# Cross-attention and feed-forward kernel on one core: a new order of its on-chip buffers, with the large ones meant to begin at multiples of 2048 bytes

## The reference

```python
x1 = layernorm(layernorm0(x), ln1_g, ln1_b)       # layernorm0: no gain, no bias
x2 = layernorm(ctx_768, ln2_g, ln2_b)
q, k, v = x1 @ Wq + bq, x2 @ Wk + bk, x2 @ Wv + bv
attn = softmax(einsum('bqe,bke->bqk', q, k) * 512 ** -0.5)
x = x + einsum('bqk,bke->bqe', attn, v) @ Wo + bo
# feed-forward; w_fc (2048 x 512), w_proj (512 x 2048), u, v of rank 16
def bitlinear(x, w):                              # ternary weights with one scale per row
    scale = max(mean(abs(w), axis=1), 1e-05)
    return x @ (clip(round(w / scale), -1, 1) * scale).T
n = layernorm0(x)
h = bitlinear(n, w_fc) + gate * (n @ v.T @ fast_b.T @ u.T)
return x + bitlinear(max(h, 0) ** 2, w_proj)
```

## Time and profile before

| | us |
|---|---|
| median of 3 runs | 861.97 |
| the 3 runs | 861.27, 861.97, 862.39 |
| time of the profiled execution | 861.97 |
| its span, from first to last instruction | 860.2 |

### The profile page before, as it was taken

One profiled execution on the slowest core, in us unless ns is written; L12 is line 12 of the kernel. 1 busy time (PEld: TensorE's weight loads), 2 busy tenths in 40 slices (PEclk: granted clock), 3 DMA queues, 4 the chain that ended last, 5 costly groups with the idle time before them and its releaser, 6 DMA issues.

```text
span 860.2 us, 11132 instructions
## 1 busy us (share of the span) xinstructions
PE 837.7 (97%) x4232; PEld 682.2 (79%) x4232; DVE 559.6 (65%) x1143; ACT 328.2 (38%) x639; POOL 137.3 (16%) x124
## 2 busy tenths in 40 slices
PE   5999789999999999999999999999999999999997
PEld 3758678888888888888888888888888888888885
DVE  4898685376836786477836786476836786476434
ACT  2687234332434234332434234333434234323332
POOL 1102140012300150012300150012300150013001
PEclk9999989999999999999999999999999999999999
DMA  9653101010111011010101011010101010000001
GB/s 326 159 151 96 38 1 49 1 37 16 41 44 37 0 50 50 1 37 24 41 35 38 1 50 50 0 37 25 53 23 37 1 49 1 1 1 25 26 0 50
DMA packets 19513, 36.55 MB, mean 42 GB/s; under 512 B 6898, under 2 KB 6898, under 8 KB 19460
## 3 DMA queue, kind: packets, MB, share of 16 engines
q1 hardware_dynamic: 18004, 35.84, 12.5%
q10 hardware_dynamic: 1456, 0.01, 0.1%
HBM read 27.45 MB, written 8.39 MB: 42 GB/s over the span
## 4 chain that ended last, share of the span: by engine, by line
PE 93%; DVE 4%; DMA 1%; issue 1%; ACT 0%; SPq 0%; POOL 0%; DVEq 0%; ACTq 0%
PE H L1114 28%; PE O L1096 27%; PE G L1014 24%; PE G L1040 3%; PE H L1120 3%; PE H L1014 1%; PE H L1040 1%; PE G L1069 1%; DMA Wk_s<-in_L_xattn_Wk_dram 1%; PE H L978 1%; PE H L998 1%; PE H L1003 0%; PE O L1135 0%; PE O L1137 0%; DVE below L913 0%
## 5 line engine op out<-in xcount | busy, mean ns | idle before, releaser
L1114 PE MATMUL H<-xnT,fcT 128*128 128x512 f32 x1024 | 263.2, 399 | 0.0
L1096 PE MATMUL O<-projT,qbuf 128*128 128x512 f32 x1008 | 257.9, 398 | 0.0
L1114 PEld LDWEIGHTS H<-xnT,fcT 128*128 128x128 f32 x1024 | 188.7, 188 | 41.9
L1096 PEld LDWEIGHTS O<-projT,qbuf 128*128 128x128 f32 x1008 | 186.3, 188 | 41.5
L646 ACT ACTIVATE qbuf<-rbuf 128x512 fp32r<-128x512 f32 x128 | 80.8, 631 | 165.5 <-DVE rbuf L887 86.5
L891 DVE TENSOR_TENSOR qbuf<-rbuf,qbuf 128x512 fp32r<-128x512 f32 x128 | 97.1, 758 | 55.6 <-ACT qbuf L646 55.6
L887 DVE TENSOR_TENSOR rbuf<-rbuf 128x512 f32<-128x512 f32 x128 | 105.6, 825 | 42.4 <-ACT rbuf L640 40.7
L640 ACT ACTIVATE rbuf<-H,scf 128x512 f32<-128x512 f32 x128 | 87.2, 681 | 93.0 <-PE H L1120 92.2
L525 POOL TENSOR_TENSOR xrs<-xrs,mhalf 128x4 f32<-128x4 f32 x9 | 9.4, 1040 | 365.1 <-DVE xrs L853 365.1
L1014 PE MATMUL G<-n1T,M 128*128 128x512 f32 x276 | 65.9, 395 | 0.0
L1014 PE MATMUL G<-Wvo,tT 128*128 128x512 f32 x270 | 65.7, 396 | 0.0
(11 more groups left out here) (158 smaller groups left out, 983.3 us busy)
## 6 DMA issues: line engine op xcount, KB each, us to landing
xb<-in_x_dram SPq DMA_DIRECT2D x8, 1024.0 KB
ctxb<-in_ctx_dram SPq DMA_DIRECT2D x8, 768.0 KB
wring<-in_L_ffn_w_fc_dram SPq DMA_DIRECT2D x16, 256.0 KB, 5.8
wring<-in_L_ffn_w_proj_dram SPq DMA_DIRECT2D x16, 256.0 KB, 3.5
out_dram<-x2a SPq DMA_DIRECT2D x8, 512.0 KB, 2.6
out_dram<-x2b SPq DMA_DIRECT2D x6, 512.0 KB, 2.6
Wq_s<-in_L_xattn_Wq_dram SPq DMA_DIRECT2D x4, 256.0 KB, 4.2
Wo_s<-in_L_xattn_Wo_dram SPq DMA_DIRECT2D x1, 1024.0 KB, 15.7
```

Source lines behind the costliest of these rows:

```text
L1096: mm = pe.matmul(banks[f"O{t}"][:, :], qbuf[:, j % 2, h, t * P:(t + 1) * P], projT[:, j, :], start=(j == 0 and h == HI), stop=(j == NFF - ...
L1114: pe.matmul(banks[f"H{j % 2}"][:, :], fcT[:, k, j * P:(j + 1) * P], xnT[:, h, k, :], start=(k == 0 and h == HI), stop=False)
```

## The change

The six large weight buffers, `sprow` and `crow` move from the head of the allocation to behind the small tiles. Between the small tiles and the large ones comes a buffer that nothing uses, `up_to_a_line`, whose length is worked out from where the allocator stands. And `absj`, a buffer of the prologue, is now another view of `sprow` instead of 2048 bytes of its own.

```diff
-        fcT = sb("fcT", [P, KD, HID], F32R)
-        projT = sb("projT", [P, NFF, D], F32R)
-        M = sb("M", [P, 2, KD, DC], F32R)
-        Wvo = sb("Wvo", [P, 2, KC, D], F32R)
-        uT = sb("uT", [P, HID], F32R)
-        FB = sb("FB", [P, KD, P], F32R)
         ident = sb("ident", [P, P])
         identb = sb("identb", [P, P], BF16)
-        sprow = sb("sprow", [P, D])
-        crow = sb("crow", [P, D])
-        bqrow = crow[:, :]
         tbias = sb("tbias", [P, KC])
...
         rinv = sb("rinv", [P, TILES])
+        LINE = 2048
+        sb("up_to_a_line", [P, (-nc.sbuf_base % LINE) // 4])
+        fcT = sb("fcT", [P, KD, HID], F32R)
+        projT = sb("projT", [P, NFF, D], F32R)
+        M = sb("M", [P, 2, KD, DC], F32R)
+        Wvo = sb("Wvo", [P, 2, KC, D], F32R)
+        uT = sb("uT", [P, HID], F32R)
+        FB = sb("FB", [P, KD, P], F32R)
+        sprow = sb("sprow", [P, D])
+        crow = sb("crow", [P, D])
         ctxb = sb("ctxb", [P, TILES, DC])
...
+        bqrow = crow[:, :]
+        absj = sprow[:, :].bitcast(BF16).rearrange("p (a d) -> p a d", a=2)
...
-        absj = sb("absj", [P, 2, D], BF16, setup)
```

## The result

| | before | after |
|---|---|---|
| median of the runs, us | 861.62 (859.85 to 862.39, 4 runs) | 847.55 (845.89 to 848.33, 4 runs) |
| ratio, 95% interval | | 0.984 (0.982 to 0.986) |
| span of the profiled execution, us | 860.2 | 846.1 |

The change made the kernel 1.6% faster.

A forecast was written before the change was run, and what follows sets the result against it. It took TensorE's rate of matmul starts, over 85% of the span, as the bound. The profiled execution's 861.97 us plus 0 for all seven parts gave 862.0 us, range 860.3 to 863.7.

The forecast's parts named there:

- What bounds the kernel: From 118 to 850 us TensorE is always busy, so the rate at which matmuls start sets the time.
- What the change does to addresses: Large buffers land 32 bytes behind multiples of 2048, not on them; three consequences for alignment and relative places follow.
- point (c): Weights and streamed operand of one matmul, 32 bytes apart within 2048 before, now stand equal or whole 512s apart.
- Part 1: Weight group's rest by 64 goes from 0 to 32 in the long matmuls: cost 0, bound 0.8 us each way.
- Part 2: Rows crossing a multiple of 2048: 512 columns still cross, halves of 256 columns swap, so units s swap times; cost 0.
- Part 3: Long matmuls with both operands at the same place: priced from units s and w, of 256 columns, at 0.
- Rival A: Equal operand places slow the long matmuls, by 0.0107 ns a column: 15 us slower, 877 us; chance 0.05.
- Rival B: The long matmuls' 20 ns over their columns are a collision the new places avoid: 56 us faster, 806 us; chance 0.02.
- Parts 4 to 7: VectorE and GpSimd with sprow and crow, VectorE in the prologue, absj as a view, and transfers: each taken as 0.
- the chance of 0.08 for a gain: Whole kernel faster by more than the 1.7 us threshold: chance 0.08, against 0.84 same and 0.08 slower.
- those of being right: In the profile after, t again 8.40 us for 36, a 4.20 for 18, "up" and "down" 1.86 to 1.87 for 8.
- those of being wrong: 8 "up" at 1.91 us or more, or 1.75 or less, or first full body over 1.7 us from 111 us.

The follow-up runs named there:

- m1_sweep: Only copies x and runs matmuls on TensorE, sweeping operand starts: 16 of 512 columns took 3.63 us at starts equal by 256 bytes, mostly 3.72 to 3.75 elsewhere.
- e9_d256: The changed kernel with the weight group at rest 32 by 2048 and the other large buffers at 288, 256 bytes further: 848.23 us.
- e1: The changed kernel with a gap buffer of the right length, so all large buffers begin at true multiples of 2048: 845.92 us, ratio 0.981.
- e2: The changed kernel without its gap, all large buffers at rest 1184 by 2048: 846.82 us, ratio 0.982.
- m2_pairs: Only copies x and runs matmuls on TensorE, with finer operand distances, pairs and column counts: long series took 3.63 us at distance 0, 3.68 to 3.81 at others.
- m3: Only copies x and runs 24 long matmuls on TensorE, some operands moved 32 or 128 bytes: a 32-byte break cost 20 to 33 ns over 3 to 5 matmuls.

## Why the prediction was wrong

**What bounds the kernel** was right: the rate of matmul starts from 118 us on is what counts, and all of the gain but 0.5 us came from it. So was the remark that an effect of addresses would have to show there.

**What the change does to addresses** was right and its point (c) named the cause, the difference of 32 bytes between streamed row and weights that becomes 0. It was put down as a matter of 2048 bytes and of 64, and the unit is 256 [m1_sweep, e9_d256].

**Part 1 (worse alignment of the weight group, 0)** had the right cost, as e1 and e2 show, and the wrong conclusion from its rows. That t and a take the same 233.3 ns shows that the roles can be swapped. It doesn't show that the difference costs nothing: it is 32 in one and 224 in the other, both out of step. No long rows with a difference of 0 stood in the trace to compare with. (Its bound is also too narrow: 0.01 us over the 18 of unit a is 0.6 ns, not 0.3.)

**Part 2 (the boundary, 0)** was right. Units s 0 and s 1 stayed at 2.15 us for 18, s 2 and s 3 went from 1.06 to 1.07 for 9, so the two did not swap, and by the prediction's own test the 1.6 ns between them before were not the boundary's. That they came from the order of the work is not shown.

**Part 3 (both operands at the same place, 0) is the step that failed.** It was worth -14 us: 14.0 us over the 2816 long matmuls, 5.0 ns each. It took its value from the units s and w, which do have equal places, as "the nearest rows". But those are of 256 columns, and up to 320 columns nothing is lost at any place tried [m1_sweep, m2_pairs], so they could say nothing. And it bounded the cost on one side only: it asked what equal places may cost, not what unequal ones were costing now. The right reading of the same numbers was there: 13.3 ns over the columns for the short ones and 20.0 for the long ones, with equal places in the first and unequal ones in the second. Rival A read this as a cost per column of being equal, which is the sign turned round.

**Rival B** had the right mechanism, a collision that the new places avoid, with a chance of 0.02. Its size was 20 ns, since it let all that is over the columns go; in t and a 6.6 of it went and 13.3 stayed, and over all 2816 it was the 5.0 ns. Against it stood that the rate doesn't depend on the slice of `fcT`. That argument was void: the slices stand 512 bytes apart, twice 256, so all of them have the same difference. And the trace of before had a row that spoke for B and that the prediction didn't weigh, the products with `uT`:

```profile
L1120 PE MATMUL H<-tstack,uT 128*128 128x512 f32 x128 | 50.2, 392 | 0.0
```

A mean of 392 ns for the same shape for which "up" has 399 is a sign that the engine can do it faster. Of their distances to the next start, 64 of the 128 were 226 or 227 ns even before. All 64 stand ahead of a product whose weights are `qbuf` or `tT`, which start at the same place by 256 as the streamed `tstack`; of the 16 ahead of a load of `fcT`, 32 bytes off, all took 231 ns or more.

**Parts 4 to 7** held. L795 (now L797) runs 675 to 693 ns, L548 (now L550) 1290 to 1750 ns, as before, the end of the chain is the same (1.29 and 1.26 us), and `absj` alone gives 1.000. The first "up" started 0.5 us earlier, which is the 72 matmuls of t and a in the prologue at 6.6 ns.

**The range** was made from the bounds of the parts, and the part that failed had been given none. The chance of 0.08 for a gain rested on the same rows. Of the signs, those of being right failed (8.16, 4.08 and 1.81 where 8.40, 4.20 and 1.86 to 1.87 were forecast), while none of those of being wrong fired: 8 "up" at 1.75 us or less would have been a gain of some 15 ns a matmul, and 5 ns on 2816 of them was enough.

## What to carry to other kernels

Where TensorE is busy without a pause, compare the distance between matmul starts at the full granted clock with columns / 2.4 GHz, over shapes and operands: an overhead that grows with the shape, or that one operand pair has and another hasn't, is a loss to be looked for. For one-pass 4-byte products of 512 columns with 128-column weights, allocate all operands so that their starts agree by 256 bytes; one small tile in between cost 1.6% of this kernel. And when "the nearest row" is to price something new, ask first whether the effect could show in that row at all.

## What the runs showed of the hardware

- A stream of 512 columns and the loads of weights beside it are not independent for this type: 226.7 ns at equal places by 256 bytes, 229 to 238 on the mean at others, in every unmixed series of full loads but one (227.0, the second at d = 240), with TensorE alone at work. The load's own mean stays at 188 to 189 ns; it is the stream that gets longer (in m1 a modelled mean of 389 to 390 ns at d = 0, 392 to 397 elsewhere). The Trainium skill says that loading the next tile's weights takes no read bandwidth from the running matmul ("TensorE: Matmul & The Clock Gate", Step-by-step: what each phase is for). For bf16 these runs show nothing against it, and for 256 columns the means stay within 118.7 to 120.0 ns. For long rows of this type, moving one matmul's weights by 32 bytes costs 20 ns (m3), so here the load is not free for the running stream. No run streams without loads, so how much of the 13.3 ns in step belongs to the load is open.
- Being in step is a state: the engine falls into it behind 1 to 12 slow distances (231, 235, 229, 232, 231 and then 227 ns, say), and transposes, short products or one operand out of place break it.
- At half the clock nothing was lost. In the stretch from 109.4 to 116.2 us (108.2 to 115.1 after the change), where the granted clock is 0.50, the products with `FB` and the first of "up" start 427 ns apart, with d = 32 before as with d = 0 after; 512 columns at 1.2 GHz are 426.7 ns. In these rows neither the 13.3 ns nor the loss out of step is there; both were seen at the granted clock of 1.00 only.
- Other lengths of load are in step at other differences (16, 48, 112, 208 for 64 columns), and outside d = 0 the same series can go either way (227.0 and 236.2 ns at 240 with full loads). Which reads meet, and why by 256, these runs leave open.
